# V made in the recurrent stage, kept in HBM and split by GpSimd

## The reference

```python
h_new = (1.0 - z) * n + z * h              # r, z, n from x @ W_ih and h @ W_hh
x1 = _ln(x) * (1.0 + scale1) + shift1
qkv = (x1 @ qkv_w + qkv_b)                 # 16 heads of 128 for Q, K and V
attn = softmax(q @ k.T * scale)            # per sequence and head, 128 x 128
x = x + gate1 * ((attn @ v) @ out_w + out_b)
x2 = _ln(x) * (1.0 + scale2) + shift2
x = x + gate2 * (gelu(x2 @ ffn_w1 + ffn_b1) @ ffn_w2 + ffn_b2)
```

## Time and profile before

| what | value |
|---|---|
| median of runs | 753.85 us (753.35 to 753.98) |
| the profiled execution's own time, by its span | 754.3 us |
| TensorE busy | 724.2 us, 96% |
| VectorE, ScalarE, GpSimd busy | 580.0, 488.7 and 104.7 us |
| HBM read, written | 16.20 MB, 2.10 MB |
| mean granted TensorE clock | 0.988 of full |

### The profile page before, as it was taken

How to read it: one execution, slowest core, us unless ns; L and a number is a source line. 1 busy time by engine, 2 the same in 40 slices (tenths; PEclk the granted TensorE clock), 3 DMA queues, 4 the chain that set the end, 5 groups by cost and what they waited for, 6 DMA issues and landing times.

```text
span 754.3 us, 25863 instructions
## 1 busy us (share of the span) xinstructions
PE 724.2 (96%) x10644; PEld 534.1 (71%) x10644; DVE 580.0 (77%) x1625; ACT 488.7 (65%) x1665; POOL 104.7 (14%) x134
## 2 busy tenths in 40 slices
PE   6899999999999989999999999999999999999997
PEld 5688888888888766767667677676676766644554
DVE  5778877888888877777778888788887888834643
ACT  4456555665565566677777677777678777766453
POOL 0322222223232210000001011010110101000040
PEclk9899998999999999999999999999999999999999
DMA  6311121111121002222222312222222231310001
GB/s 234 102 45 45 46 69 63 45 46 44 46 62 55 3 16 43 44 43 42 46 43 43 50 37 56 38 50 44 44 43 43 43 49 37 48 25 28 29 1 56
DMA packets 77869, 36.75 MB, mean 49 GB/s; under 512 B 70539, under 2 KB 73783, under 8 KB 77751
## 3 DMA queue, kind: packets, MB, share of 16 engines
q1 hardware_dynamic: 77175, 33.52, 19.5%
q10 hardware_dynamic: 576, 1.57, 0.6%
HBM read 16.20 MB, written 2.10 MB: 24 GB/s over the span
## 4 chain that ended last, share of the span: by engine, by line
PE 83%; DVE 6%; DMA 4%; ACT 3%; issue 2%; SPq 2%; DVEq 0%; POOL 0%; POOLq 0%
PE bank L428 20%; PE bank L430 19%; PE bank L429 19%; PE bank L535 12%; PE bank L543 5%; PE bank L448 4%; DMA pT_lo<-p_lo 3%; DVE h_hi L1210 2%; SPq L307 2%; ACT zg L936 1%; DVE nu L1204 1%; PE bank L435 1%; PE bank L464 1%; PE bank L457 1%; DMA x<-in_x 0%
## 5 line engine op out<-in xcount | busy, mean ns | idle before, releaser
L428 PE MATMUL bank<-y_hi,w_hi 128*128 128x512 f16 (+2 forms) x496 | 140.6, 301 | 0.3 <-DVE qk_lo L1187 0.2
L430 PE MATMUL bank<-y_lo,w_hi 128*128 128x512 f16 (+2 forms) x496 | 140.8, 302 | 0.0
L429 PE MATMUL bank<-y_hi,w_lo 128*128 128x512 f16 (+2 forms) x496 | 140.7, 302 | 0.0
L535 PE MATMUL bank<-h_hi,whh_hi 128*128 128x16 f16 x1536 | 110.9, 173 | 14.1 <-DVE h_hi L1210 11.7
L535 PEld LDWEIGHTS bank<-h_hi,whh_hi 128*128 128x128 f16 x1536 | 89.5, 96 | 36.7 <-DVE h_hi L1210 34.5
L996 ACT ACTIVATE prob<-bank,nmx 128x128 f32<-128x128 f32 x256 | 90.4, 366 | 29.7 <-DVE nmx L1285 29.7
L535 PE MATMUL bank<-h_hi,whh_lo 128*128 128x16 f16 x1536 | 108.7, 172 | 0.0
L535 PEld LDWEIGHTS bank<-h_hi,whh_lo 128*128 128x128 f16 x1536 | 90.0, 96 | 0.1
L428 PE MATMUL bank<-w_hi,y_hi 128*128 128x128 f16 x512 | 89.1, 219 | 0.5 <-DVE v_lo L1289 0.5
L429 PE MATMUL bank<-w_hi,y_lo 128*128 128x128 f16 x512 | 89.1, 219 | 0.0
L430 PE MATMUL bank<-w_lo,y_hi 128*128 128x128 f16 x512 | 89.1, 219 | 0.0
(11 more groups left out here) (156 smaller groups left out, 2161.6 us busy)
## 6 DMA issues: line engine op xcount, KB each, us to landing
stage<-in_weights SPq DMA_DIRECT2D x16, 640.0 KB, 3.9
x<-in_x SPq DMA_DIRECT2D x16, 128.0 KB, 3.8
out<-xr SPq DMA_DIRECT2D x3, 512.0 KB, 3.1
xr<-in_ada_r SPq DMA_DIRECT2D x1, 1024.0 KB, 7.6
pT_hi<-p_hi SPq DMA_TRANSPOSE x64, 2.4
pT_lo<-p_lo SPq DMA_TRANSPOSE x64, 2.5
xr<-in_W_ih ACTq DMA_DIRECT2D x2, 384.0 KB, 3.8
xr<-in_W_hh ACTq DMA_DIRECT2D x2, 384.0 KB, 5.8
```

Of the source, the lines that this page charges most:

```text
L428: mm(ps, w[0], a[0], start=start, stop=False, skip_group_check=True)
L429: mm(ps, w[1], a[0], start=False, stop=False, skip_group_check=True)
L430: return mm(ps, w[0], a[1], start=False, stop=stop, skip_group_check=True)
L535: nc.tensor.matmul(out(m0 + m), half[:, k, (m0 + m) * P:(m0 + m + 1) * P], h_hi[:, k * B:(k + 1) * B, 1], start=False, stop=False, skip_gr ...
```

## The change

V of all heads is no longer made in the loop. Two heads at a time (`value_item`: 6 matmuls of 256 columns for the 8 time steps and 16 sequences of a block) it is made in the recurrent stage, one item in most steps from step 14 on, 109 items; the last 19 follow behind the last step. ScalarE copies each item in f32 from PSUM to `v_rows` (behind the last step VectorE takes every other one), SP stores half a block's rows (512 KB) to `v_spill` in HBM, and loads 256 KB per head in the loop. GpSimd makes both halves of V from the load (`value_split`). The items for Q and K ahead are gone: all 64 heads make Q and K in the loop. `y_hi` and `y_lo` are laid out by block, and the second layer norm's halves lie where the first weights were (`x2_hi`, `x2_lo`). `four`, `prob`, `p_hi`, `p_lo` and `pT` have two buffers each; project_out lags by 4; its PSUM banks alternate by group, and the layer norm reads PSUM without a copy (`norm_copy` is gone). GpSimd's layer norm work stands in its loop between the wait for `s_pn` and the next split.

```diff
-AHEAD = (0, 6, 8, 14)
...
-LAG = 3
...
+PAIRS = H // 2
+VP = 2 * DH
+SIDE = INNER // 2
+SLOTS = [(2, head) for head in range(H)] + [(which, head) for head in range(H) for which in range(2)]
+def value_items():
+    first = [(0, 0), (0, 1), (0, 2), (0, 3), (0, 4), None, None, None, (1, 0), (1, 1), (0, 5), (1, 2), (1, 3),
+             (0, 6), None, None, (0, 7), (1, 4), (1, 5), (1, 6), (1, 7)]
+    order, place = [], {}
+    for i, item in enumerate(first):
+        if item:
+            place[BS + 6 + i] = len(order)
+            order.append(item)
+    at = BS + 6 + len(first)
+    for n in range(2, NBL - 2):
+        for pair in range(PAIRS):
+            if at < T:
+                place[at] = len(order)
+                at += 1
+            order.append((n, pair))
+    order += [(NBL - 2, pair) for pair in range(PAIRS // 2)] + [(NBL - 1, pair) for pair in range(PAIRS // 2)]
+    order += [(NBL - 2, pair) for pair in range(PAIRS // 2, PAIRS)]
+    order += [(NBL - 1, pair) for pair in range(PAIRS // 2, PAIRS)]
+    return order, place
+VITEMS, VPLACE = value_items()
+VTAIL = len(VPLACE)
+def by_scalar(i):
+    return i < VTAIL or i % 2 == 0
+def taken(i):
+    scalar = sum(by_scalar(j) for j in range(i + 1))
+    return scalar, i + 1 - scalar
+def piece_of(pair):
+    return -(-(pair + 1) * VP * KD // PC)
+LAG = 4
...
+GATE, RESIDUAL = {4: 0, 6: 1}, {5: 0, 7: 1}
+FORWARD, BACK, HIGH = {7: 0, 8: 1}, {12: 0, 13: 1}, {14: 0, 15: 1}
...
+REST, SUM, LOW = {9: 0, 10: 1}, {12: 0, 13: 1}, {0: 0, 1: 1}
...
+        v_spill = nc.dram_tensor("v_spill", (T, B, INNER), f32).ap()
...
+            def store_values(n, side):
+                last = VITEMS.index((n, (side + 1) * PAIRS // 2 - 1))
+                scalar, vector = taken(last)
+                sp.wait_ge(v_act, scalar)
+                if vector > 0:
+                    sp.wait_ge(v_dve, vector)
+                sp.dma_start(v_spill[n * BS:(n + 1) * BS, :, side * SIDE:(side + 1) * SIDE].rearrange("t b c -> b t c"),
+                             v_rows[:, n % 2, side, :]).then_inc(v_out[n % 2][side], 16)
...
+                if r > 2:
+                    store_values(r - 3, 1)
+                if r > 1:
+                    store_values(r - 2, 0)
+            store_values(NBL - 4, 1)
+            store_values(NBL - 3, 0)
+            store_values(NBL - 3, 1)
+            store_values(NBL - 2, 0)
+            store_values(NBL - 1, 0)
...
+            def load_values(d):
+                g, head = d // H, d % H
+                if d > 1:
+                    sp.wait_ge(v_l, d - 1)
+                sp.dma_start(v_full[:, d % 2, :].rearrange("p (j c) -> p j c", j=QUAD),
+                             v_spill[:, g * QUAD:(g + 1) * QUAD, head * DH:(head + 1) * DH]).then_inc(v_in[d % 2], 16)
+            for n in (NBL - 2, NBL - 1):
+                sp.wait_ge(v_out[n % 2][0], 16 * (NBL // 2))
+            load_values(0)
+            load_values(1)
+            turn(0)
+            for d in range(1, HEADS):
                 turn(d)
+                if d < 3:
+                    store_values(NBL - 3 + d, 1)
+                if d + 1 == H // 2:
+                    for n in (NBL - 2, NBL - 1):
+                        sp.wait_ge(v_out[n % 2][1], 16 * (NBL // 2))
+                if d + 1 < HEADS:
+                    load_values(d + 1)
...
+            def value_split(d):
+                pool.wait_ge(v_in[d % 2], 16 * (d // 2 + 1))
+                if d > 2:
+                    pool.wait_ge(a_mm, d - 2)
+                nc.gpsimd.tensor_copy(v_hi[:, d % 3, :], v_full[:, d % 2, :]).then_inc(v_h, 1)
+                pool.wait_ge(v_h, d + 1)
+                gtt(v_lo[:, d % 3, :], v_full[:, d % 2, :], v_hi[:, d % 3, :], sub).then_inc(v_l, 1)
+            for d in range(HEADS):
+                if d >= H and (d + 1) % H == VAR:
+                    norm_rstd(d // H - 1)
+                value_split(d)
+                g, i = (d + 2) // H, (d + 2) % H
+                if d + 2 < HEADS:
+                    pool.wait_ge(s_pn, d + 3)
+                if g > 0 and i in REST:
+                    bias_rest(g - 1, REST[i])
+                if g > 0 and i in SUM:
+                    sum_rest(g - 1, SUM[i])
+                if g > 1 and i in LOW:
+                    norm_low(g - 2, LOW[i])
...
+            def value_item(i):
+                n, pair = VITEMS[i]
+                pe.wait_ge(lb_lo, n + 1)
+                if n == 0:
+                    pe.wait_ge(piece_lo, piece_of(pair))
+                scalar, vector = taken(i)
+                if by_scalar(i) and scalar > 1:
+                    pe.wait_ge(v_act, scalar - 1)
+                elif vector > 1:
+                    pe.wait_ge(v_dve, vector - 1)
+                ps = v_bank(i).rearrange("p (h c) -> p h c", c=DH)
+                heads = slice(2 * pair, 2 * pair + 2)
+                for k in range(KD):
+                    mm = product(ps, (y_hi[:, k, n, :], y_lo[:, k, n, :]),
+                                 (wq_hi[:, heads, k, :], wq_lo[:, heads, k, :]), k == 0, k == KD - 1)
+                mm.then_inc(v_mm, 1)
...
-            share = (0, 0, 7, 9, 22, 25, 31, 32, 36)
+            share = (0, 0, 2, 9, 16, 23, 27, 33, 36)
...
+                    if t1 - 1 in VPLACE:
+                        value_item(VPLACE[t1 - 1])
...
-            def values(d):
-                g, head = d // H, d % H
-                if d > 0:
-                    pe.wait_ge(v_l, d)
-                else:
-                    pe.wait_ge(qk_l, LAST["old"] + 1)
-                w = SLOTS.index((2, head))
-                for j in range(QUAD):
-                    for k in range(KD):
-                        mm = product(bank[2][:, j * DH:(j + 1) * DH],
-                                     (y_hi[:, k, g * QUAD + j, :], y_lo[:, k, g * QUAD + j, :]),
-                                     (wq_hi[:, w, k, :], wq_lo[:, w, k, :]), j == 0 and k == 0, k == KD - 1)
-                mm.then_inc(v_mm, 1)
...
             def attend(d):
-                pe.wait_ge(p_turn, 32 * (d + 1))
-                if d == 0:
-                    pe.wait_ge(qk_l, LAST[1] + 1)
+                pe.wait_ge(p_turn[d % 2], 32 * (d // 2 + 1))
+                pe.wait_ge(v_l, d + 1)
...
+            tall_parts(tall_rest, 1, 1, before)
+            tall_parts(tall_rest, 1, 0, last).then_inc(q_mm, 1)
+            tall_parts(tall_rest, 1, 1, last).then_inc(k_mm, 1)
+            for i in range(VTAIL + 5, VTAIL + 7):
+                value_item(i)
...
+            for i in range(VTAIL + 7, VTAIL + 11):
+                value_item(i)
+            pe.wait_ge(piece_lo, NBL * PB)
+            queries(2)
             scores(1)
-            ahead(LAST["rest"])
-            pe.wait_ge(piece_lo, NBL * PB)
-            values(1)
+            value_item(VTAIL + 11)
+            value_item(VTAIL + 12)
+            keys(2)
+            value_item(VTAIL + 13)
+            value_item(VTAIL + 14)
             queries(3)
             scores(2)
             attend(0)
-            values(2)
+            value_item(VTAIL + 15)
+            value_item(VTAIL + 16)
             keys(3)
-            project_out(0)
+            value_item(VTAIL + 17)
+            value_item(VTAIL + 18)
+            queries(4)
             attend(1)
-            queries(4)
-            values(3)
             scores(3)
-            for d in range(4, HEADS):
+            for d in range(LAG, HEADS):
                 g, i = d // H, d % H
-                late = g > 0 and i == LAG
-                if i not in AHEAD:
-                    keys(d)
-                else:
-                    queries(d + 1)
-                if i in AHEAD or a_late(d - 1):
-                    values(d)
-                if not late:
-                    project_out(d - LAG)
-                if i not in AHEAD and not a_late(d - 1):
-                    values(d)
-                attend(d - 2)
+                keys(d)
+                project_out(d - LAG)
                 if g > 0 and i in FORWARD:
                     pair_rows(g - 1, FORWARD[i])
                 if g > 0 and i in BACK:
                     pair_back(g - 1, BACK[i])
-                if d == HEADS - 1:
-                    pe.wait_ge(q_l, len(WHOLE))
+                if d < HEADS - 1:
+                    queries(d + 1)
+                else:
+                    pe.wait_ge(q_l, HEADS)
                     up(0)
-                elif i not in AHEAD and (d + 1) % H not in AHEAD:
-                    queries(d + 1)
-                if late:
-                    project_out(d - LAG)
+                attend(d - 2)
                 scores(d)
-                if d in (5, 8):
-                    ahead(LAST[2 if d == 5 else 3])
+            project_out(HEADS - 4)
+            up(1)
+            up(2)
...
+            def value_out(i):
+                n, pair = VITEMS[i]
+                act.wait_ge(v_mm, i + 1)
+                if n > 1:
```

(68 more changed lines are left out.)

463 lines of the change are left out of this document (192 added, 271 removed).

## The result

The changed kernel takes 892.59 us (median of 4 runs, 891.26 to 894.90) against 753.91 for the kernel before (753.35 to 755.25): a ratio of 1.1837, interval 1.1811 to 1.1863. It is slower by 139 us where 109 were forecast, inside the range. The profiled execution's span is 890.2 us, 135.9 above that of before.

A forecast was written before the change was run, and what follows sets the result against it. A closed ring of softmax, GpSimd's split, attend and scores was taken to bound the loop; 754.3 + 73.3 (loop) + 21 (recurrent stage) + 12.7 (head) + 2.5 (tail) = 863.8 profiled, so 863 us; range 820 to 915.

The forecast's parts named there:

- The ring: Attention loop: closed chain of softmax, split, attend and scores once an iteration, 7.11 us (bounds 6.51 to 8.22).
- X: Length of GpSimd's split in the loop: cast 0.55, gap 0.15, subtraction 1.16, VectorE meeting 0.2; 2.06 us, bounds 1.46 to 3.17.
- GpSimd's layer norm work: Loop: bias_rest, sum_rest, norm_low and norm_rstd between the s_pn wait and the split lengthen the loop by 21.6 us.
- The recurrent stage: Steps before attention: value items' matmuls fill the steps, ScalarE's copies delay the sigmoid; +21 us, bounds zero and 33 plus 15.
- I add 0.2 to X: Loop: prob_low on VectorE falls on GpSimd's subtraction and lengthens the split by 0.2 us; bounds zero and 0.6.
- the second rival: Loop: the shared SBUF port as an exclusive lock; X 2.46, 24 us more, 887 us in all; chance 13%.
- the fifth rival: Loop: TensorE drops to its lower clock, 1.2 instead of 2.4 GHz; above 1050 us in all; chance 3%.
- Into the slack at nothing: Loop: layer norm transposes, residuals and gate evacuations fit the slack of TensorE and other engines; cost nothing.
- The 7 us for ScalarE: Recurrent stage: ScalarE's copy with weight casts behind it delays the sigmoid of r, 0.6 us a block, 7 us.
- The fourth rival: Recurrent stage: ScalarE's copy falls into every step, +0.3 on 93 steps less the 7 counted; 885 us; chance 8%.
- The head: Last step to iteration 4: more TensorE work, attend(0) waits for head 0's split; 30 us, +12.7, bounds +9 and +19.
- The first rival: Loop: split hidden, TensorE's 5.22 us an iteration bound it; -57 us, 732 us in all; chance 5%.

The follow-up runs named there:

- experiment 1: Changed kernel with GpSimd's wait for s_pn at d+2 instead of d+3, so each split starts one head earlier: 759.52 us, ratio 1.0065.
- experiment 2: Changed kernel with the subtraction that makes v_lo done twice, the second behind the first: 991.64 us (one run).
- experiment 4: Changed kernel with p_lo made from K's PSUM bank instead of prob, ahead of K's low half (p's low half wrong): 856.12 us, ratio 1.1342.
- experiment 6: Changed kernel with GpSimd's wait on s_nm (scaled maximum) of d+2 instead of s_pn of d+3: 757.56 us, ratio 1.0018.
- experiment 8: Changed kernel with GpSimd waiting for s_nm of d+3, and bias_rest, sum_rest and norm_low ahead of that wait: 740.78 us, ratio 0.9807.
- experiment 11: Changed kernel with three of the six matmuls of a value item in the recurrent steps (V incomplete): 879.43 us (one run).
- experiment 10: Changed kernel with ScalarE copying 8 of 256 columns of a value item in the recurrent steps, from the 17th item: 890.39 us (one run).
- experiment 7: Changed kernel with GpSimd's wait on s_nm (scaled maximum) of d+3 instead of s_pn of d+3: 747.79 us, ratio 0.9891.

## Why the prediction was right, and where its sizes were off

**The ring** was right in its place, its order and its 5.05 us of fixed length (5.08). Experiment 1 shows that it is what bounds the loop, experiment 2 that X counts in it one to one. Of the signs that the prediction named, TensorE stands still 2.02 us for 1.9, the maxima are 7.41 apart for 7.1, and GpSimd's pair takes 2.33 for 1.9 to 2.1; the page names no releaser, and the late recurrent blocks, at 16.60, lie below the 16.8 to 17.6.

The loop is 31.9 us longer than forecast: 18.0 are the ring's own length (7.41 for 7.11, nearly all of it X), 12.8 TensorE's clock, 2.3 the gates and 0.5 GpSimd's layer norm work, less 1.7 in the split. That the whole is nearer, 892.6 for 863, is partly luck: the recurrent stage was priced 8.5 us too dear.

**X was mis-sized, in the term for the shared port.** The cast is 0.61 (0.55 forecast), the gap 475.73 to 475.81 is 0.08 (0.15), the subtraction alone 1.15 (1.16): together 1.84 for 1.86. What failed is "I add 0.2 to X": p_lo starts 0.06 ahead of the subtraction and costs it 0.49, as experiment 4 shows by taking it away. The price stood in the feed-forward rows from which the 0.2 came. There the row of 2.48 us holds two bias_rest, and the prediction took half of it, 1.24, for each. One by one they are not alike:

```profile
724.76 0.79 DVE L1326 TENSOR_TENSOR four<-nat,four 128x512 f16<-128x512 f32 x1 [1.90 <-ACT four L1032]
...
724.96 1.49 POOL L393 TENSOR_TENSOR xr<-xr,gb 128x512 f32<-128x512 f32 x1
726.41 1.04 POOL L393 TENSOR_TENSOR xr<-xr,gb 128x512 f32<-128x512 f32 x1
```

The first meets a VectorE subtraction and takes 0.45 more, the second meets none. With 0.49 in place of 0.2 the prediction's own sum makes the ring 7.40. 60 times 7.41-7.11 is 18 us of the loop's miss.

The Trainium skill ("SBUF — State Buffer", section Who interferes with whom) says that the engine which comes second to the shared port pair is blocked for the whole instruction of the first. The traces agree, but for 0.13 to 0.16 us: in each of these rows the second takes its own time and what is left of the first, less that much.

| second instruction, its start | alone | left of the first | took |
|---|---|---|---|
| bias_rest, 724.96, kernel before | 1.04 | 0.59 | 1.49 |
| sum_rest, 727.40, kernel before | 1.26 | 0.64 | 1.76 |
| VectorE's subtraction, 729.94, kernel before | 0.69 | 0.44 | 1.00 |
| v_lo, 475.81 | 1.15 | 0.63 | 1.64 |
| norm_rstd, 491.92 | 1.02 | 0.59 | 1.47 |
| scaling, 425.91, experiment 1 | 0.17 | 1.08 | 1.09 |
| scaling, 402.66, experiment 6 | 0.17 | 0.73 | 0.76 |

So the second rival had the mechanism; its X, 2.46, lies 0.13 above the 2.33.

**GpSimd's layer norm work** was priced by its rows at 21.6, and its sixteen iterations are 30.2 longer. The work itself was priced well: between the normalized rows and the split it takes 22.1. Its one surprise is norm_rstd, 1.47 where it had taken 1.02, again behind p_lo:

```profile
490.92 1.04 POOL L475 TENSOR_TENSOR xr<-xr,gb 128x512 f32<-128x512 f32 x1 [5.09 <-DVE prob L1323]
491.54 0.97 DVE L1328 TENSOR_TENSOR p_lo<-prob,p_hi 128x512 f16<-128x512 f32 x1
491.92 1.47 POOL L464 TENSOR_TENSOR rstd<-veps,nhalf 128x4 f32<-128x4 f32 x1
```

The split itself is 1.8 shorter over these iterations, mostly in the three with norm_rstd, where p_lo is over before it (0.60 and 1.15). What the price lacked is 9.9 us of TensorE's clock.

**The clock** stood in the sum at nothing, and as the fifth rival at half speed throughout; it came in part. The loop's granted clock was 1.00 before and is 0.93 after, with a standstill of 2.0 us in every 7.4; it is back at 1.00 in experiment 8, where TensorE is busy 323 of 329 us. Of TensorE's work only attend and scores are links of the ring. From attend's first matmul to the next maximum, at full clock and at 0.50, the lower of the two levels:

```profile
477.55:479.09 1.54, 1.54 (x25) 1.44 (x26) 0.00 (x1) 0.67 (x1) 0.00 (x0) 1.00 0.45 89
495.29:498.05 2.76, 2.76 (x25) 2.66 (x26) 0.01 (x1) 0.69 (x1) 0.00 (x0) 0.50 0.34 101
```

Over the sixty iterations this stretch is 12.8 us longer than sixty times 1.54: 9.9 in the iterations with layer norm work, 0.7 in the gates' and 2.3 in the six without other work. What else the lower clock costs is hidden in the standstill, as the iteration of 7.41 at 0.85 shows. Why the lower clock falls on attend in some iterations and not in others was not tested.

**"Into the slack at nothing"** was wrong for the gates: 3.0 us in six iterations at 7.79 to 8.25, of which 0.7 are the clock. In the 7.79 ScalarE's four gate instructions run from 440.96 to 442.46, and the exponentials behind them start at 442.33, 0.39 behind the scaled maximum's end, for 0.03 in the plain iteration above: the maximum to the normalized rows takes 3.75 us instead of 3.37.

**The recurrent stage** cost 12.55 where 21 were forecast. The matmul term, 14.5, is near: without half of the matmuls the last state comes 14.0 earlier (experiment 11). The 7 us for ScalarE failed: with the short copy it comes 0.65 earlier (experiment 10). Of eight steps one is longer on its account, 2.05 us instead of 1.96: 0.1 a block instead of 0.6. The fourth rival falls with it. The other two steps whose fill was priced at 1.04 stayed at 1.96.

**The head** took 32.6 for 30, in part for a queue that the prediction had not followed:

```profile
298.81 1.64 SPq L380 DMA_DIRECT2D v_full<-v_spill  x2
...
301.86 1.26 SPq L373 DMA_TRANSPOSE pT_lo<-p_lo  x1
...
302.49 1.15 POOL L492 TENSOR_TENSOR v_lo<-v_full,v_hi 128x512 f16<-128x512 f32 x1
...
304.43 0.23 PE L520 MATMUL bank<-pT_hi,v_hi 128*128 128x128 f16 x1 [3.13 <-DMA pT_lo<-p_lo]
```

attend(0) starts 24.4 us behind the last state, not 22.5. The split of head 0, for which the sum had it wait, ends at 303.64, 23.6 behind the last state. The other 0.8 are the first transposes of p: their data was there by 296, but they stand on SP behind the two loads, and those wait for the store.

**Stores and loads** in the loop cost nothing, as forecast (256 KB land in 2.9 us). Experiment 6 shows what this rested on: with the split an iteration earlier the same load is late.

**The first rival**, the split hidden, had its count right: experiment 7 runs at its 5.22 us an iteration. What it lacked is the wait, which in the changed kernel stands one head too late and on the wrong event.

## What to carry to other kernels

When work moves to an idle engine, follow its in-order queue: the wait that stands ahead of the work, not the engine's load, decides whether its length costs anything, and a wait on an event of the next iteration can close a ring through the bound engine. When GpSimd is given work beside VectorE, ask which VectorE instruction it will meet each time round; here a four-element scaling on the critical path stood up to 0.92 us for its own 0.17, and tying the split to the event just behind it (experiment 7) was worth 12 us over tying it to the rows (experiment 1). A load issued in order behind transposes is only as early as they are. Where a row of a timeline holds two instructions, look at each by itself before you take the mean as a price: 2.48 for two was 1.49 and 1.04. And compare stages only when both kernels are cut at the same event.

## What the runs showed of the hardware that was not expected

- Where GpSimd and VectorE meet, the second waits for the first almost to its end, whichever of the two it is: GpSimd's subtraction goes from 1.15 to 1.64 us behind p_lo, a VectorE scaling of 4 elements from 0.17 to 1.09 behind GpSimd's subtraction, in both cases its own time and what is left of the first, less 0.13 to 0.16. A start 0.06 earlier is enough to be first. With one of p_lo's operands in PSUM both run at their own speed (0.69 and 1.15, experiment 4).
- The same stretch of TensorE's work, attend and scores, takes 1.54 us at a granted clock of 1.00 and 2.76 at 0.50; in the loop this costs time only where that stretch itself falls on the lower clock.
- GpSimd starts a cast of 512 elements 0.07 us behind the VectorE instruction that releases it, and the subtraction 0.08 behind its own cast: its waits cost little here, its meetings with VectorE up to 0.50.
